# The down projection of a ViT tower layer in pairs of token blocks with seven block products, its fourth row sum on GpSimd

## The chip, the core and the metric

One core of one Trainium2 chip runs the whole program as one launch. The metric is the device time of one execution in microseconds (us), from its first to its last instruction and what lies around them. Three executions of the kernel before gave 1929.54, 1930.83 and 1933.36 us; their median, 1930.83 us, is the time before.

The engines are named as in the profile: PE (TensorE, matmuls) with PEld (its weight loads), DVE (VectorE), ACT (ScalarE), POOL (GpSimd), and SP (SyncE), whose queue issues the DMAs.

## What is computed

16 sequences of 128 tokens and 1024 features run through a state-space kernel, one attention block and one gated feed-forward block. The change is in the last step of the feed-forward block, the projection `down`:

```python
def _qlinear(x, q, scale, A, Bm):
    w = (q.astype(jnp.float32) - Q_ZERO) * (scale * Q_STEP)[:, None]
    y = jnp.einsum('bsh,oh->bso', x, w)
    return y + LR_SCALE * (x @ A @ Bm)
g = _qlinear(x, gate_q, gate_scale, gate_A, gate_B)
u = _qlinear(x, up_q, up_scale, up_A, up_B)
h = jax.nn.silu(g) * u
return _qlinear(h, down_q, down_scale, down_A, down_B)   # 2752 -> 1024, levels 0..15
```

The layer's output is that plus the residual `h1`.

## The kernel before

**Tiling.** `C` = 16 blocks of `P` = 128 tokens, n = 0 to 15. The 2752 hidden features are `IT` = 22 tiles of 128 rows, of which the first `FULL` = 21 come in two f16 parts (high and low, whose sum is the f32 value) and the last, half a tile with both parts stacked, in one. So a block is 43 weight tiles, and each is multiplied with the two halves of 512 output columns: 86 matmuls of 128x128 by 128x512 in f16. `levels[i]` is tile i of the quantised weights less 7.5, f16, held in SBUF in the rooms of `x_hi`, `x_lo` and `down_levels`. `parts[n % 3]` holds block n of the hidden values, 1376 KB, loaded from `hidden_parts` in DRAM.

**The stage.** Before it, the gate and up projections run as a loop over 42 jobs, each of which after the fourth is itself made of seven half products (`half_features`), with sums of tokens and of levels made by DVE, ACT and POOL beside the matmuls. The down stage then runs over n. PE does `down(n, ...)`: 86 matmuls into the two PSUM banks of `acc[n % 2]`, with `low_term(n)` (2 matmuls in f32, the low-rank term, to `ps_l`) in their midst, and raises `s_main`. ACT turns the low-rank term into `lrt[n % 2]` (`down_term`, line 1830). POOL adds the residual `h1d` to it (line 1162). DVE multiplies the sums by the column scales into `y[n % 2]` (line 2270) and adds `lrt` (line 2273), and SP stores `y`. In the last block the two halves of the columns come one after the other.

**Order.** Every engine's program is written out by hand; engines wait for one another by semaphores. PE starts block n when its parts have landed and DVE has read the bank (`s_y1`). SP loads parts n + 3 when block n's matmuls are done, then the residual n + 2, then stores y n. DVE reads operands either from PSUM (`acc`, `ps_l`) or from SBUF (all others); POOL works in SBUF alone. A helper `Chain` lets an instruction wait for the one before it on the same engine.

## Time and profile before

| | |
|---|---|
| median of 3 runs | 1930.83 us |
| the profiled execution's own time | 1929.66 us |
| its span, first to last instruction | 1927.9 us |
| PE busy | 1805.6 us, 94% of the span |
| DVE busy | 1197.5 us, 62% |
| POOL busy | 859.1 us, 45% |
| ACT busy | 712.6 us, 37% |
| down stage, first to last matmul | 1618.0 to 1923.9 us of the span |

Busy shares are means over stages that differ: in the down stage DVE, ACT and POOL have each less than an eighth of the time filled, in the gate and up stage POOL has more than half. In the rows below, a line such as `1667.27 18.58 PE acc L1514 x86` is a start time, a length, an engine, what it writes, the line of the kernel and the number of instructions taken together. "idle before" is the time for which the engine stood still ahead of an instruction, with what ended it.

### The profile page before, as it was taken

How to read it: one execution, taken by the hardware profiler on the slowest of the kernel's cores; microseconds unless marked ns; L12 is line 12 of the kernel's file. 1: busy time of each engine (PE TensorE's matmuls, PEld its weight loads, DVE VectorE, ACT ScalarE, POOL GpSimd, SP SyncE). 2: the span in 40 equal slices, each digit the busy share in tenths (PEclk: the TensorE clock that was granted, in tenths of full speed). 3: DMA queues.
4: the chain of work that ended last, by engine and by line, in shares of the span. 5: the costliest groups of instructions: out<-in, count | busy, mean ns of one | idle time of the engine just before them, and what ended most of it. 6: DMA issues, size and time to landing. Idle time of an engine off the chain costs nothing.

```text
span 1927.9 us, 31412 instructions
## 1 busy us (share of the span) xinstructions
PE 1805.6 (94%) x12892; PEld 984.2 (51%) x12892; DVE 1197.5 (62%) x1570; ACT 712.6 (37%) x1026; POOL 859.1 (45%) x593
## 2 busy tenths in 40 slices
PE   0586999999999999999999999999999999999999
PEld 0575665656666655545554344444444444444444
DVE  8996577787878888855656876675755554111111
ACT  4477243343433344432114645454544443000000
POOL 6973134343333434432361577664777774011111
PEclk9998999999999999999999999999999999999999
DMA  2122111111122221144532343434465454434341
GB/s 97 43 67 68 62 56 22 34 37 43 47 58 64 80 75 63 67 147 163 168 121 67 98 132 99 131 113 139 142 195 172 156 164 147 154 106 150 113 143 44
DMA packets 102704, 194.92 MB, mean 101 GB/s; under 512 B 14305, under 2 KB 75489, under 8 KB 92065
## 3 DMA queue, kind: packets, MB, share of 16 engines
q1 hardware_dynamic: 102560, 192.90, 31.2%
q8 instruction: 103, 1.69, 0.4%
q14 instruction: 41, 0.33, 0.1%
HBM read 135.72 MB, written 56.11 MB: 100 GB/s over the span
## 4 chain that ended last, share of the span: by engine, by line
PE 75%; DVE 9%; POOL 2%; issue 2%; ACT 2%; DMA 0%; DVEq 0%; ACTq 0%
PE acc L1514 15%; PE acc L1380 12%; PE acc L1382 12%; PE ps_p L1172 4%; PE ps_p L1174 4%; PE ps_p L1173 4%; PE acc L1286 3%; PE acc L1287 3%; PE ps_t L1199 3%; PE acc L1288 3%; PE ps_p L1188 2%; PE ps_p L1190 2%; PE ps_p L1189 2%; PE ps_l L1389 2%; POOL prob L1061 1%
## 5 line engine op out<-in xcount | busy, mean ns | idle before, releaser
L1061 POOL TENSOR_TENSOR prob<-prob,mx 128x1024 f32<-128x1024 f32 x64 | 121.4, 1897 | 371.5 <-DVE mx L1883 371.5
L1172 PE MATMUL ps_p<-x_hi,w_qk 128*128 128x512 f16 x512 | 194.7, 380 | 0.0
L1173 PE MATMUL ps_p<-x_lo,w_qk 128*128 128x512 f16 x512 | 194.0, 379 | 0.0
L1174 PE MATMUL ps_p<-x_hi,w_qk 128*128 128x512 f16 x512 | 194.0, 379 | 0.0
L2270 DVE TENSOR_TENSOR y<-acc,down_scale 128x1024 f32<-128x1024 f32 (+1 forms) x17 | 19.7, 1162 | 253.0 <-PE acc L1514 253.0
L1114 POOL TENSOR_TENSOR hidden<-up,hidden 128x512 f16<-128x512 f32 x80 | 91.1, 1160 | 144.8 <-ACT hidden L1740 144.6
L1162 POOL TENSOR_TENSOR lr_term<-lr_term,h_again 128x1024 f32<-128x1024 f32 x16 | 37.6, 2347 | 253.6 <-ACT lr_term L1830 253.6
L1188 PE MATMUL ps_p<-w_v,x_hi 128*128 128x256 f16 x512 | 140.5, 274 | 4.8 <-PEq L806 3.6
L1066 POOL TENSOR_TENSOR prob<-prob,sm 128x1024 f32<-128x1024 f32 x64 | 120.2, 1897 | 52.9 <-DVE sm L1890 52.9
L1189 PE MATMUL ps_p<-w_v,x_hi 128*128 128x256 f16 x512 | 140.4, 274 | 0.0
L1190 PE MATMUL ps_p<-w_v,x_lo 128*128 128x256 f16 x512 | 140.4, 274 | 0.0
L1574 ACT ACTIVATE pth<-ps_t 128x512 f16<-128x512 f32 x128 | 76.1, 595 | 163.8 <-PE ps_t L1199 163.7
L2135 DVE SCALAR_TENSOR_TENSOR up<-acc,gu_scale,up 128x512 f32<-128x512 f32 x120 | 90.0, 750 | 61.2 <-PE acc L1382 60.1
L258 PE MATMUL ssm_ps<-phase,magnitude 128*128 128x128 f32 x512 | 67.1, 288 | 65.0 <-DVE magnitude L469 61.9
L2135 DVE SCALAR_TENSOR_TENSOR gate<-acc,gu_scale,gate 128x512 f32<-128x512 f32 x120 | 89.6, 747 | 56.2 <-PE acc L1382 55.4
L1380 PE MATMUL acc<-x_hi,q_sums 128*128 128x512 f16 x320 | 121.7, 380 | 1.1 <-issue 0.8
L1380 PE MATMUL acc<-x_sum,q_sums 128*128 128x512 f16 x320 | 121.3, 379 | 0.0
L1382 PE MATMUL acc<-x_sum,q_sums 128*128 128x512 f16 x320 | 121.3, 379 | 0.0
L1380 PE MATMUL acc<-x_hi,q_f 128*128 128x512 f16 x320 | 121.3, 379 | 0.0
L1382 PE MATMUL acc<-x_lo,q_f 128*128 128x512 f16 x320 | 121.3, 379 | 0.0
L1382 PE MATMUL acc<-x_lo,q_sums 128*128 128x512 f16 x320 | 121.3, 379 | 0.0
L1894 DVE SCALAR_TENSOR_TENSOR ptl<-ps_t,pth 128x512 f16<-128x512 f32 x128 | 87.7, 685 | 47.4 <-ACT pth L1574 46.9
(343 smaller groups left out, 4367.7 us busy)
## 6 DMA issues: line engine op xcount, KB each, us to landing
q_raw<-in_gu_q SPq DMA_DIRECT2D x42, 1024.0 KB, 6.2
hid_parts<-hidden_parts SPq DMA_DIRECT2D x16, 1376.0 KB, 6.7
hidden_parts<-hidden SPq DMA_DIRECT2D x42, 512.0 KB, 3.5
down_raw<-in_down_q SPq DMA_DIRECT2D x22, 512.0 KB, 3.6
w_raw<-in_w_qk SPq DMA_DIRECT2D x8, 1024.0 KB, 5.0
h_tokens<-n_tok SPq DMA_DIRECT2D x16, 512.0 KB, 3.7
o_parts<-ot SPq DMA_DIRECT2D x32, 256.0 KB, 2.3
wv_raw<-in_w_o SPq DMA_DIRECT2D x8, 1024.0 KB, 4.8
```

The lines of the kernel that those rows point to most:

```text
L1061: nc.gpsimd.tensor_tensor(prob[s % 2][p][:], prob[s % 2][p][:], bc(mx[p][:], H, 2), ALU.subtract).then_inc(s_sub[p], 1)
L1066: nc.gpsimd.tensor_tensor(prob[s % 2][p][:], prob[s % 2][p][:], bc(sm[p][:], H, 2), ALU.mult).then_inc(s_prob[p], 1)
L1172: nc.tensor.matmul(out[:], w[:, j % 2, m, 0, at], xn_hi[:, k, tok], start=(k == 0), stop=False)
L1173: nc.tensor.matmul(out[:], w[:, j % 2, m, 0, at], xn_lo[:, k, tok], start=False, stop=False)
L1174: last = nc.tensor.matmul(out[:], w[:, j % 2, m, 1, at], xn_hi[:, k, tok], start=False, stop=(k == KT - 1))
L1188: nc.tensor.matmul(out, xn_hi[:, k, tok], wv[:, g % 2, 0, at], start=(k == 0), stop=False)
L1189: nc.tensor.matmul(out, xn_hi[:, k, tok], wv[:, g % 2, 1, at], start=False, stop=False)
L1190: last = nc.tensor.matmul(out, xn_lo[:, k, tok], wv[:, g % 2, 0, at], start=False, stop=(k == KT - 1))
L1380: nc.tensor.matmul(banks[bank], lev[:, k * P:(k + 1) * P], hi[:, k, :], start=(k == 0 and not adds), stop=False, skip_group_check=adds)
L1382: last = nc.tensor.matmul(banks[bank], lev[:, k * P:(k + 1) * P], lo[:, k, :], start=False, stop=(k == KH - 1), skip_group_check=adds)
L1514: last = nc.tensor.matmul(acc[n % 2][:, b, :], parts[n % 3][:, at], levels[i][:, b * CH:(b + 1) * CH], start=(i == 0 and part == 0), stop= ...
L2135: stt(to[:], banks[bank], scl[:, m, i:i + 1], to[:], ALU.mult, ALU.add).then_inc(s_read, 1)
```

## The change

Blocks 0 and 1 are done as before. Blocks 2 to 15 are done in seven pairs, q = 1 to 7, block n = 2q and block m = 2q + 1. Of the 22 tiles the first 20 are cut in two halves of `KD` = 10, the columns in two halves of 512, and the pair's 2 x 2 x 2 block products of these tiles are made from seven: p1, p2, p6, p5, p7, p3, p4, each 20 matmuls. The tiles 20 and 21 (3 matmuls for a block and half) are done plainly (`down_rest`): p22 is one of them, the others follow within p2, p3 and p4.

For that there are new sums. Of the levels, four per tile, made once (`level_sum`, in f16, 128x512): the first on DVE (ten), the third on POOL (ten), the second six on DVE and the last `BY_POOL` = 4 on POOL, the fourth on DVE (ten). Of the hidden values, four for each pair, in two pieces h of 128x640 in f32: the first and the third on POOL (`hid_one`, `hid_three`, three instructions a piece), the second on DVE (`sum_two_hid`, two a piece), the fourth on POOL (`hid_four`, two a piece, in place in the second's room). Each piece is then copied to a high f16 part by ACT (`high_hid_sum`) and its low part made by DVE (`low_hid_sum`). ACT also copies p1 to SBUF (`first_down`), so that p2 can be added to it in its bank. DVE reads the banks seven times a pair (c11, x22, v, x5, x7, c12, c21), and scaling is a step of its own for three of the four quarters.

There are four rooms for parts in place of three, one for the residual in place of two. In the last pair the columns' right half ends first. Two powers of two change in `hid_up` and `hid_down`; they move no instruction.

The diff, cut to its core:

```diff
...
+KD = 10
+DP = C // 2
...
+BY_POOL = 4
...
-            sp.dma_start(parts[n % 3][:], hid_dram[n, :, :]).then_inc(s_parts[n % 3], 16)
+            sp.dma_start(parts[n % 4][:], hid_dram[n, :, :]).then_inc(s_parts[n % 4], 16)
...
+        def next_residual(n):
+            sp.wait_ge(s_sum, n + 1)
+            sp.dma_start(h1d[:], h1_dram[n + 1, :, :]).then_inc(s_h1d, 16)
+        def store_rows(n):
             sp.wait_ge(s_y, n + 1)
             sp.dma_start(out[n, :, :], y[n % 2][:]).then_inc(s_yout[n % 2], 16)
...
+        for q in range(DP):
+            next_residual(2 * q)
+            if q + 2 < DP:
+                if q:
+                    sp.wait_ge(s_dprod, dprod(q, "p3"))
+                else:
+                    sp.wait_ge(s_main, 1)
+                load_parts(2 * q + 4)
+                if q:
+                    sp.wait_ge(s_dprod, dprod(q, "p4"))
+                else:
+                    sp.wait_ge(s_main, 2)
+                load_parts(2 * q + 5)
+            store_rows(2 * q)
+            if q + 1 < DP:
+                next_residual(2 * q + 1)
+                store_rows(2 * q + 1)
...
-        for n in range(C):
-            pool.wait_ge(s_h1d[n % 2], 16 * (n // 2 + 1))
+        def residual_and_term(n):
+            pool.wait_ge(s_h1d, 16 * (n + 1))
             pool.wait_ge(s_lrt, n + 1)
-            nc.gpsimd.tensor_tensor(lrt[n % 2][:], lrt[n % 2][:], h1d[n % 2][:], ALU.add).then_inc(s_sum, 1)
+            tt(lrt[n % 2][:], lrt[n % 2][:], h1d[:], ALU.add).then_inc(s_sum, 1)
+        def hid_one(q, h):
...
...
+            chain.after(tt(to[:], hid_piece(2 * q + 1, 0, h, 0), hid_piece(2 * q + 1, 1, h, 0), ALU.add))
+            chain.after(tt(to[:], to[:], hid_piece(2 * q + 1, 0, h, 1), ALU.add))
+            tt(to[:], to[:], hid_piece(2 * q + 1, 1, h, 1), ALU.add).then_inc(s_f1, 1)
+        def hid_three(q, h):
...
...
+            chain.after(tt(to[:], hid_piece(2 * q, 0, h, 0), hid_piece(2 * q + 1, 0, h, 0), ALU.subtract))
+            chain.after(tt(to[:], to[:], hid_piece(2 * q, 0, h, 1), ALU.add))
+            tt(to[:], to[:], hid_piece(2 * q + 1, 0, h, 1), ALU.subtract).then_inc(s_f3, 1)
+        def hid_four(q, h):
...
+            chain.after(tt(to[:], hid_piece(2 * q, 1, h, 0), to[:], ALU.subtract))
+            tt(to[:], to[:], hid_piece(2 * q, 1, h, 1), ALU.add).then_inc(s_f4, 1)
+        pool.wait_ge(s_prod, PROD.total)
+        for i in range(KD):
+            tt(level_sum(3, i), level_block(1, 1, i), level_block(0, 1, i), ALU.subtract).then_inc(s_l3, 1)
+        for q in range(DP):
+            if q:
+                hid_four(q, 0)
+                hid_four(q, 1)
+            if q + 1 < DP:
+                hid_one(q + 1, 0)
+                hid_one(q + 1, 1)
+                hid_three(q + 1, 0)
+            residual_and_term(2 * q)
+            if q == 0:
+                pool.wait_ge(s_half, 1)
+                for i in range(KD - BY_POOL, KD):
+                    pool.wait_ge(s_l1, i + 1)
+                    pool.wait_ge(s_l3, i + 1)
+                    tt(level_sum(2, i), level_sum(3, i), level_block(0, 0, i), ALU.add).then_inc(s_l2_pool, 1)
+            if q + 1 < DP:
+                hid_three(q + 1, 1)
+            residual_and_term(2 * q + 1)
...
+        down(1, 0, KD).then_inc(s_half, 1)
+        low_term(1)
+        down(1, KD, IT).then_inc(s_main, 1)
...
+        for q in range(1, DP):
+            n, m = 2 * q, 2 * q + 1
...
+            if q == 1:
+                pe.wait_ge(s_y1, 1)
+            else:
+                pe.wait_ge(s_dread, dread(q - 1, "c11"))
+            down_block(0, lambda i, part: hid_part(n, i, part), lambda i: level_block(0, 0, i), False, True).then_inc(s_dprod, 1)
             low_term(n)
...
-        low_term(C - 1)
...
+            if q == 1:
+                pe.wait_ge(s_y1, 2)
+            else:
+                pe.wait_ge(s_dread, dread(q - 1, "x22"))
+            down_rest(3, m, 1, False).then_inc(s_dprod, 1)
...
+            down_block(0, lambda i, part: hid_part(n, KD + i, part), lambda i: level_block(1, 0, i), True, False)
+            down_rest(0, n, 0, True).then_inc(s_dprod, 1)
+            pe.wait_ge(s_dl[1], 2 * q)
+            if q == 1:
+                pe.wait_ge(s_l2, KD - BY_POOL)
+                pe.wait_ge(s_l2_pool, BY_POOL)
+            else:
+                pe.wait_ge(s_dread, dread(q - 1, "c21"))
+            down_block(1, lambda i, part: dsum[1][part][:, i, :], lambda i: level_sum(2, i), False, True).then_inc(s_dprod, 1)
+            pe.wait_ge(s_dl[0], 2 * q)
+            if q == 1:
+                pe.wait_ge(s_l1, KD)
+            else:
+                pe.wait_ge(s_dread, dread(q - 1, "c12"))
+            down_block(2, lambda i, part: dsum[0][part][:, i, :], lambda i: level_sum(1, i), False, True).then_inc(s_dprod, 1)
+            pe.wait_ge(s_dl[2], 2 * q)
+            if q == 1:
+                pe.wait_ge(s_l3, KD)
+            pe.wait_ge(s_dread, dread(q, "v"))
+            down_block(1, lambda i, part: dsum[2][part][:, i, :], lambda i: level_sum(3, i), True, True).then_inc(s_dprod, 1)
+            pe.wait_ge(s_dl[3], 2 * q)
+            pe.wait_ge(s_dread, dread(q, "x5"))
+            down_block(2, lambda i, part: dsum[3][part][:, i, :], lambda i: level_block(1, 1, i), True, False)
+            down_rest(2, n, 1, True).then_inc(s_dprod, 1)
+            low_term(m)
+            if q == 1:
+                pe.wait_ge(s_l4, KD)
+            pe.wait_ge(s_dread, dread(q, "x7"))
+            down_block(1, lambda i, part: hid_part(m, KD + i, part), lambda i: level_sum(4, i), True, False)
+            down_rest(1, m, 0, True).then_inc(s_dprod, 1)
...
-        for n in range(C):
-            down_term(n)
+        def high_hid_sum(q, k, h, src, made):
+            act.wait_ge(made, 2 * (q - 1) + h + 1)
+            if q > 1:
+                act.wait_ge(s_dprod, dprod(q - 1, ("p5", "p6", "p7", "p3")[k]))
+            nc.scalar.activation(piece(dsum[k][0], h), src[:], ACT.Copy).then_inc(s_dh[k], 1)
+        def first_down(q):
+            act.wait_ge(s_dprod, dprod(q, "p1"))
+            if q > 1:
+                act.wait_ge(s_dread, dread(q - 1, "c21"))
+            nc.scalar.activation(first_d[:], acc[0][:, 0, :], ACT.Copy).then_inc(s_dfirst, 1)
+        act.wait_ge(s_prod, PROD.total)
+        for q in range(DP):
+            if q:
+                for h in two:
+                    high_hid_sum(q, 2, h, f3[h], s_f3)
+                first_down(q)
+            down_term(2 * q)
+            if q:
+                for h in two:
+                    high_hid_sum(q, 3, h, f2[h], s_f4)
+            if q + 1 < DP:
+                for h in two:
+                    high_hid_sum(q + 1, 1, h, f2[h], s_f2)
+                for h in two:
+                    high_hid_sum(q + 1, 0, h, f1[h], s_f1)
+            down_term(2 * q + 1)
...
+        def low_hid_sum(q, k, h, src):
+            dve.wait_ge(s_dh[k], 2 * (q - 1) + h + 1)
+            tt(piece(dsum[k][1], h), src[:], piece(dsum[k][0], h), ALU.subtract).then_inc(s_dl[k], 1)
+        def sum_two_hid(q, h):
...
+            dve.wait_ge(s_f1, 2 * (q - 1) + h + 1)
...
...
+            chain.after(tt(to[:], f1[h][:], hid_piece(2 * q, 0, h, 0), ALU.subtract))
+            tt(to[:], to[:], hid_piece(2 * q, 0, h, 1), ALU.subtract).then_inc(s_f2, 1)
+        def sum_down(q, name, product, bank, to, other, behind):
+            dve.wait_ge(s_dprod, dprod(q, product))
+            if behind:
+                dve.wait_ge(s_dread, dread(q, behind))
+            tt(to, banks[bank], other, ALU.add).then_inc(s_dread, 1)
...
+        def add_term(n, cols):
+            chain.wait()
             dve.wait_ge(s_sum, n + 1)
             tt(y[n % 2][:, cols], y[n % 2][:, cols], lrt[n % 2][:, cols], ALU.add).then_inc(s_y, 1)
+        def last_down(q):
+            sum_down(q, "c21", "p4", 1, y[1][:, left], first_d[:], None)
...
+            scaled(y[1], left)
...
+        dve.wait_ge(s_prod, PROD.total)
+        for i in range(KD):
+            tt(level_sum(1, i), level_block(0, 1, i), level_block(0, 0, i), ALU.subtract).then_inc(s_l1, 1)
         dve.wait_ge(s_dscl, 16)
         ts(scl_d[:], scl_d[:], down_scale[:], None, ALU.mult).then_inc(s_dscl2, 1)
+        dve.wait_ge(s_low, LOWS.total)
         dve.wait_ge(s_dscl2, 1)
-        for n in range(C - 1):
-            scale_sums(n, 0, False)
...
+        scale_sums(0)
+        for h in two:
+            sum_two_hid(1, h)
+        dve.wait_ge(s_half, 1)
+        for i in range(KD - BY_POOL):
+            dve.wait_ge(s_l3, i + 1)
+            tt(level_sum(2, i), level_sum(3, i), level_block(0, 0, i), ALU.add).then_inc(s_l2, 1)
+        scale_sums(1)
+        for k in (1, 0):
+            for h in two:
+                low_hid_sum(1, k, h, (f1, f2)[k][h])
+        add_first(0)
+        add_first(1)
+        for i in range(KD):
+            if i < KD - BY_POOL:
+                dve.wait_ge(s_l2, i + 1)
+            else:
+                dve.wait_ge(s_l2_pool, i + 1 - (KD - BY_POOL))
+            tt(level_sum(4, i), level_block(1, 0, i), level_sum(2, i), ALU.subtract).then_inc(s_l4, 1)
+        for q in range(1, DP):
+            if q > 1:
+                last_down(q - 1)
+                add_term(2 * q - 1, slice(0, D))
+            for h in two:
+                low_hid_sum(q, 2, h, f3[h])
+            for h in two:
+                low_hid_sum(q, 3, h, f2[h])
...
+            dve.wait_ge(s_dprod, dprod(q, "p2"))
+            tt(y[0][:, left], banks[0], scl_d[:, left], ALU.mult).then_inc(s_dread, 1)
...
+            sum_down(q, "x22", "p22", 3, y[1][:, right], first_d[:], None)
+            if q + 1 < DP:
+                sum_two_hid(q + 1, 0)
+            sum_down(q, "v", "p6", 1, y[0][:, right], first_d[:], None)
+            if q + 1 < DP:
+                sum_two_hid(q + 1, 1)
+                low_hid_sum(q + 1, 1, 0, f2[0])
+            sum_down(q, "x5", "p5", 2, y[1][:, right], y[1][:, right], "x22")
+            if q + 1 < DP:
+                for h in two:
+                    low_hid_sum(q + 1, 0, h, f1[h])
+                low_hid_sum(q + 1, 1, 1, f2[1])
+            sum_down(q, "x7", "p7", 1, y[1][:, right], y[1][:, right], "x5")
...
+            scaled(y[1], right)
+            sum_down(q, "c12", "p3", 2, y[0][:, right], y[0][:, right], "v")
...
+            scaled(y[0], right)
+            add_term(2 * q, slice(0, D))
+        add_term(C - 1, right)
+        last_down(DP - 1)
+        add_term(C - 1, left)
...
```

On DVE, in the first pair, this stands between the last hidden values of the gate and up stage and the first blocks' end before:

```order
L2193 TENSOR_TENSOR inner_stack1_2028<-ps_i1,inner_stack1_2028 32x512 [waits f_iact] x2
L2278 TENSOR_SCALAR down_scale_2038<-down_scale_2038,g_down_scale_1950 128x1024 [waits f_dscl]
L2270 TENSOR_TENSOR y0_2034<-acc0,down_scale_2038 128x1024 [waits f_main,f_dscl2]
L2273 TENSOR_TENSOR y0_2034<-y0_2034,lr_term0_2032 128x1024 [waits f_sum,f_y1]
L2270 TENSOR_TENSOR y1_2035<-acc1,down_scale_2038 128x1024 [waits f_main]
L2273 TENSOR_TENSOR y1_2035<-y1_2035,lr_term1_2033 128x1024 [waits f_sum,f_y1]
```

And now on DVE, from the second level sum (L2520) on; `hid_f20` and `hid_f21` are the two pieces of the second hidden sum, `hid_sum11` the low part of the second, `hid_sum21` of the third, L2532 the fourth level sum:

```order
L2520 TENSOR_TENSOR x_hi_64<-x_hi_64 128x512 [waits f_level_sum3] x5
L2462 TENSOR_TENSOR y1_2051<-acc1,down_scale_2053 128x1024 [waits f_main]
L2471 TENSOR_TENSOR hid_sum11_2036<-hid_f20_2043,hid_sum10_2035 128x640 [waits f_sum_hi2]
L2471 TENSOR_TENSOR hid_sum11_2036<-hid_f21_2044,hid_sum10_2035 128x640 [waits f_sum_hi2]
L2471 TENSOR_TENSOR hid_sum01_2034<-hid_f10_2041,hid_sum00_2033 128x640 [waits f_sum_hi1]
L2471 TENSOR_TENSOR hid_sum01_2034<-hid_f11_2042,hid_sum00_2033 128x640 [waits f_sum_hi1]
L2467 TENSOR_TENSOR y0_2050<-y0_2050,lr_term0_2048 128x1024 [waits f_sum,f_y1]
L2467 TENSOR_TENSOR y1_2051<-y1_2051,lr_term1_2049 128x1024 [waits f_sum,f_y1]
L2532 TENSOR_TENSOR x_lo_65<-x_lo_65,x_hi_64 128x512 [waits f_level_sum2] x6
L2532 TENSOR_TENSOR x_lo_65<-down_levels_2022,x_hi_64 128x512 [waits f_level_sum2_pool] x2
L2532 TENSOR_TENSOR x_lo_65<-down_levels_2022,x_lo_65 128x512 [waits f_level_sum2_pool] x2
L2471 TENSOR_TENSOR hid_sum21_2038<-hid_f30_2045,hid_sum20_2037 128x640 [waits f_sum_hi3]
```

The reading of block 1's bank (L2462) now stands behind the second level sums, and the low part for p7 (`hid_sum21`) behind all ten fourth level sums.

On POOL, at the end of the gate and up stage and the start of the down stage, before:

```order
L1118 TENSOR_SCALAR down_levels_2022<-down_raw_2023 128x1024 [waits g_lraw]
L1114 TENSOR_TENSOR hidden0_1975<-up01_1961,hidden0_1975 128x4x128 [waits g_hhi,d_xlo]
L1114 TENSOR_TENSOR hidden0_1975<-up00_1960,hidden0_1975 128x4x128 [waits g_hhi]
L1114 TENSOR_TENSOR hidden1_1976<-up11_1963,hidden1_1976 128x4x128 [waits g_hhi]
L1114 TENSOR_TENSOR hidden1_1976<-up10_1962,hidden1_1976 128x4x128 [waits g_hhi]
L1162 TENSOR_TENSOR lr_term0_2032<-lr_term0_2032,h1_again0_2036 128x1024 [waits f_lrt,f_h1d0]
L1162 TENSOR_TENSOR lr_term1_2033<-lr_term1_2033,h1_again1_2037 128x1024 [waits f_lrt,f_h1d1]
```

And now on POOL in an inner pair, from the end of the first hidden sum to the start of the next pair's fourth (`hid_f30` and `hid_f31` are the pieces of the third, `hid_f20` one of the fourth):

```order
L1234 TENSOR_TENSOR hid_f11_2042<-hid_f11_2042,hid_parts3_2032 128x640 [waits a_out0]
L1242 TENSOR_TENSOR hid_f30_2045<-hid_parts2_2031,hid_parts3_2032 128x640 [waits f_sum_lo3,f_parts2]
L1243 TENSOR_TENSOR hid_f30_2045<-hid_f30_2045,hid_parts2_2031 128x640 [waits a_out0]
L1244 TENSOR_TENSOR hid_f30_2045<-hid_f30_2045,hid_parts3_2032 128x640 [waits a_out0]
L1223 TENSOR_TENSOR lr_term0_2048<-lr_term0_2048,h1_again_2052 128x1024 [waits f_lrt,f_h1d]
L1242 TENSOR_TENSOR hid_f31_2046<-hid_parts2_2031,hid_parts3_2032 128x640 [waits f_sum_lo3,f_parts2]
L1243 TENSOR_TENSOR hid_f31_2046<-hid_f31_2046,hid_parts2_2031 128x640 [waits a_out0]
L1244 TENSOR_TENSOR hid_f31_2046<-hid_f31_2046,hid_parts3_2032 128x640 [waits a_out0]
L1223 TENSOR_TENSOR lr_term1_2049<-lr_term1_2049,h1_again_2052 128x1024 [waits f_lrt,f_h1d]
L1251 TENSOR_TENSOR hid_f20_2043<-hid_parts2_2031,hid_f20_2043 128x640 [waits f_parts2,f_sum_lo2]
```

A queue that held one instruction a block now holds nine a block; the residual's addition stands between the two pieces of the third sum.

## Rows read from the trace of the kernel before

**Rows 1.** The page: engine, busy us (share) xinstructions; then busy tenths in 40 slices.
```profile
PE 1805.6 (94%) x12892; PEld 984.2 (51%) x12892; DVE 1197.5 (62%) x1570; ACT 712.6 (37%) x1026; POOL 859.1 (45%) x593
...
PE   0586999999999999999999999999999999999999
```

**Rows 2.** Chain that ended last, in order of time, down stage: start, us, what.
```profile
1633.05 0.45 PE ps_l L1526 x2
...
1648.22 18.58 PE acc L1514 x86
1666.80 0.47 PE ps_l L1526 x2
```

**Rows 3.** The same chain's end.
```profile
1910.08 13.85 PE acc L1514 x64
1923.92 0.02 issue
1923.95 0.70 DVE y L2270
```

**Rows 4.** Busy time by stretch; a busy time (xcount) for each engine, clock, DMA.
```profile
core 0: us, PE busy (x) PEld busy (x) DVE busy (x) ACT busy (x) POOL busy (x), PEclk, DMA share, GB/s
182.00:191.00 9.00, 3.57 (x16) 2.77 (x14) 2.61 (x3) 4.63 (x7) 0.00 (x0) 0.50 0.06 25
191.00:195.00 4.00, 3.24 (x16) 2.35 (x17) 2.56 (x5) 0.00 (x0) 0.00 (x0) 0.50 0.55 180
196.00:200.00 4.00, 4.00 (x39) 3.59 (x38) 2.50 (x2) 0.60 (x1) 0.00 (x0) 1.00 0.05 4
1648.00:1905.00 257.00, 257.00 (x1189) 117.61 (x1189) 31.93 (x27) 15.60 (x14) 32.87 (x14) 1.00 0.36 119
```

**Rows 5.** Groups by line and shape: count | busy, mean ns | idle before.
```profile
L1162 POOL TENSOR_TENSOR lr_term<-lr_term,h_again 128x1024 f32<-128x1024 f32 x16 | 37.6, 2347 | 253.6 <-ACT lr_term L1830 253.6
L2273 DVE TENSOR_TENSOR y<-y,lr_term 128x1024 f32<-128x1024 f32 x15 | 18.4, 1225 | 0.5
L2273 DVE TENSOR_TENSOR y<-y,lr_term 128x512 f32<-128x512 f32 x2 | 1.4, 692 | 0.1
L2278 DVE TENSOR_SCALAR down_scale<-down_scale,g_down_scale 128x1024 f32<-128x1024 f32 x1 | 0.8, 753 | 1.1 <-DMA down_scale<-in_down_scale 1.1
L1830 ACT ACTIVATE lr_term<-ps_l,g_down_back 128x1024 f32<-128x1024 f32 x16 | 17.8, 1114 | 263.6 <-PE ps_l L1526 263.6
```

**Rows 6.** Lines of the gate and up stage: min/median/max ns.
```profile
L1106 POOL TENSOR_TENSOR q_sums<-q_f x40: 1145/1154/1163, 1064.4 to 1600.2; 128x512 f16<-128x512 f16 x40
L1747 ACT ACTIVATE x_sum<-sum x24: 612/619/631, 1030.1 to 1284.2; 128x512 f16<-128x512 f32 x24
L2175 DVE TENSOR_TENSOR sum<-sum,x_hi x8: 681/1159/1639, 1038.2 to 1262.4; 128x512 f32<-128x512 f32 x8
```

**Rows 7.** Timeline, POOL, gate and up stage: start, us, instruction.
```profile
1151.94 1.16 POOL L1108 TENSOR_TENSOR q_sums<-q_f 128x512 f16<-128x512 f16 x1
1153.05 1.60 POOL L1109 TENSOR_TENSOR q_sums<-q_f,q_sums 128x512 f16<-128x512 f16 x1
```

**Rows 8.** The same stretch on DVE.
```profile
1152.03 0.75 DVE L2135 SCALAR_TENSOR_TENSOR up<-acc,gu_scale,up 128x512 f32<-128x512 f32 x1 [0.32 <-PE acc L1382]
1152.70 0.94 DVE L2154 TENSOR_TENSOR x_sum<-sum,x_sum 128x512 f16<-128x512 f32 x1
1153.56 1.64 DVE L2175 TENSOR_TENSOR sum<-sum,x_hi 128x512 f32<-128x512 f32 x1
1155.23 0.69 DVE L2176 TENSOR_TENSOR sum<-sum,x_lo 128x512 f32<-128x512 f32 x1
```

**Rows 9.** Timeline, DVE, first stage: a 640-element instruction, and one beside POOL.
```profile
67.65 0.82 DVE L459 TENSOR_TENSOR phase<-a,c_im 128x640 f32<-128x640 f32 x1
68.39 2.95 DVE L465 TENSOR_TENSOR v_second<-w_v 128x1024 f32<-128x1024 f32 x1
```

**Rows 10.** DMA issues of the down stage: xcount, KB each, median us to landing.
```profile
hid_parts<-hidden_parts SPq DMA_DIRECT2D x15, 1376.0 KB, 6.6
```

**Rows 11.** Timeline, PE, 181 to 192: matmuls after an idle time.
```profile
186.17 1.97 PE L275 MATMUL n_pn<-ident,magnitude 128*128 128x128 f32 x8 [2.57 <-ACT magnitude L342]
191.76 0.37 PE L1188 MATMUL ps_p<-w_v,x_hi 128*128 128x256 f16 x1 [3.62 <-PEq L806]
```

131 lines of the change are left out of this document (92 added, 39 removed).

## The prediction, as it stood before the run

> **What bounds the kernel now.** Read the page first: PE is busy for 94% of the span and for nine tenths or more of every slice after the fourth [rows 1]. Then the chain of waits in order of time: through the down stage it is PE alone, 86 matmuls in 18.58 us and two f32 ones of the low-rank term in 0.47 us, block after block [rows 2], so 0.216 us a matmul and 38.10 us for two blocks. The busy times by stretch say the same: 257 us of 257 for PE at the full clock, and 31.9 us for DVE, 15.6 for ACT, 32.9 for POOL [rows 4]. Only the number of matmuls can shorten this stage, as long as the other three keep up. The last matmul starts 0.38 us before 1923.92; behind it lie DVE's two instructions of 0.7 us and a store [rows 3].
>
> **What is removed.** A pair takes 7 x 20 + 3 + 3 x 3 = 152 matmuls where two blocks took 172, and the same 4 f32 ones: 152 x 0.216 + 2 x 0.47 = 33.8 us for 38.1. Seven pairs: 140 x 0.216 = **30.2 us less**. That part is certain.
>
> **What is added, per inner pair.** POOL: 16 instructions of 640 elements and the two additions of 1024. One of 512 takes 1.154 us [rows 6], one of 1024 2.347 [rows 5], so one of 640 1.45, and 16 x 1.45 + 2 x 2.35 = 27.9 us, with some 0.8 us between chained ones. DVE: 12 of 640 from SBUF at 0.82 [rows 9], three scalings of 512 at 0.69 and two additions of 1024 at 1.23 [rows 5], seven readings of a bank at about 0.69: 9.8 + 2.1 + 2.5 + 4.8 = 19.2 us. ACT: 8 copies of 640 at about 0.72 (0.62 for 512 [rows 6]), one of 512 and two of 1024 at 1.11 [rows 5]: 8.6 us. Each alone fits into 33.8 us. If that were all, the work would hide behind PE.
>
> **What speaks against it: DVE and POOL stop one another.** In the gate and up stage POOL's L1108 ends at 1153.10 [rows 7]. DVE's L2154, begun at 1152.70, has two SBUF operands and takes 0.94 in place of 0.68 us [rows 8]. POOL's next takes 1.60 in place of 1.16 [rows 7], and DVE's next, L2175, 1.64 [rows 8] where its shortest is 0.681 [rows 6]. They take turns: from POOL's end at 1153.10 to its next at 1154.65 are 1.55 us, of which POOL works some 1.02 and DVE 0.53. L2135, one of whose operands is in PSUM, is not held up beside the same POOL instructions: 0.75 [rows 8]. The first stage shows it again, 2.95 us for an instruction of 1024 elements [rows 9]. In the down stage it is not seen, because POOL and DVE have one short instruction each a block, at different times. The change puts 17 DVE instructions with two SBUF operands into each pair beside 18 of POOL.
>
> The Trainium skill has this as a rule (SBUF — State Buffer, section SBUF: two separate sides): the port pair that the two share is taken for a whole instruction, and the loser fully blocks. By the rule's letter a turn of two 512s would be 1.16 + 0.69 = 1.85 us, where the trace shows 1.55; the measurement decides, and with 1.85 the sum below would be some 30 us higher.
>
> Scaled to 640 elements a turn is 1.31 + 0.68 = **1.99 us**, the price of each of the 12 while POOL is kept busy. An addition of 1024 costs 1.08 + 1.31 = 2.4 us, a scaling between 0.69 and 1.9, say 1.2. DVE's inner pair is then 12 x 1.99 + 2 x 2.4 + 3 x 1.2 + 7 x 0.61 (readings back to back) = 36.6 us, and 0.8 us of waits for POOL that find no filler: **37.4 us**. POOL's is about the same, 16 turns of 1.99 and the additions. So neither hides behind 33.8 us; PE waits ahead of p3 and p4, whose banks DVE has to read first. Five inner pairs (q = 2 to 6): **17.9 us more**. The last pair has no next one to prepare, and runs at PE's pace. The bounds: with 1.40 and 0.78 us for the 640s a pair is 36.2, with 1.50 and 0.82 it is 38.2, so 12 to 22 us.
>
> **The first pair.** Zero is the first down matmul, 1618.0. I lay DVE's queue out from there. POOL makes the ten third level sums until 16, waits for parts 3, which SP issues at 8 behind other loads (6.6 us and more to landing [rows 10]), until about 20, and has the first piece at 24.6. DVE then does four instructions of the second hidden sum, with a wait of 1.4 for the second piece (to 34.0), six level sums f16 from f16 in turns with POOL (9.9), block 1's bank (1.2), four low parts (7.8, one behind an addition of POOL's), the additions of blocks 0 and 1 (4.8), ten fourth level sums (14.5, eight in turns), four low parts (5.4), two bank readings (1.2), two sums for pair 2 (3.7) and v (0.6): it ends at **83.0**. p7 waits for v. At PE's pace p7 would start at 39.05 + 4.3 + 0.5 + 0.6 + 5.0 + 4.3 + 4.3 = 58.1. Of the 25.0 us between, 1.3 are lost ahead of p22 (block 1's bank), 4.9 ahead of p2 (ACT's copy of p1 stands behind the high part of the third sum's second piece, which POOL finishes at 48.6) and 18.8 ahead of p7. With 1.6 us ahead of p3: **26.6 us more**.
>
> An f16 level sum alone is not in the trace. Between 0.38 (half of DVE's 1024 elements of one operand in 0.753 [rows 5]) and 0.69 for two [rows 5] I take the middle, 0.53, as no row is nearer; the ends are 2.4 us less and 3.0 more. The Trainium skill (VectorE: DVE Perf Modes, section The perf-mode tier table) gives two-operand 16-bit instructions in SBUF twice the rate; an estimate from its formula is 0.42 us, and the sum would be 1.8 us lower. No run here shows it yet. Landings 1 us a load sooner or later move this pair by 2 us down or 4 up.
>
> **The clock.** After 9 us in which PE was busy for 3.57, and a wait of 3.62 us [rows 4, 11], the granted clock stood at 0.50 from 191 to 195 and at 1.00 from 196 [rows 4]. A wait of 18.8 us should do that at least once: about 4 us at half pace, **2 us**, between 0 and 4.
>
> **The tail.** p4 is followed by three DVE instructions where two stood, 0.7 us, and its bank is the last: with the hand-overs **1.0 us**.
>
> **The sum.** -30.2 + 17.9 + 26.6 + 2.0 + 1.0 = **+17.3 us**. The profiled execution took 1929.66 us, 1.2 under the median; 1947.0 on that, **1948** on the median of 1930.83. The loss is made in the first pair, and the inner pairs gain only 0.7 us each on what stood before (37.4 for 38.1).
>
> **Rivals.**
> *The engines don't stop one another here.* Faster. If turns cost nothing, DVE's 19 and POOL's 28 us hide, and the first pair has only 3 us of waits, for parts 3 and POOL's sums: -30.2 + 3 + 1 = -26, 1905 us. For it: each engine's own sum is under 33.8. Against it: rows 7 to 9, in two stages. Its point of decision is the low parts' duration, 0.82 or about 2 us. 7%.
> *The turns are real, but half hidden.* If POOL's waits for landings and for the low-rank term leave DVE free, an inner pair is 35 and the first one 52: -30.2 + 6 + 18 + 2 = -4, 1927. For it: POOL has 8 to 9 us of waits in the first pair. Against: they fall at its end, behind the queue. 11%, half of it faster by over 0.2%, half the same.
> *POOL is the bound.* If its instructions on strided f16 pieces take 1.6 us, or three and more turns fall into one addition, an inner pair is 40 and the first 66: -30.2 + 31 + 32 + 4 + 1 = +38, 1969. For it: nothing in [rows 6], where a strided form is absent. 9%.
> *It doesn't do what it says.* The two new powers of two and the rooms move no instruction, and the order of the instructions shows the seven products; under 1%, in the others.
>
> **How the numbers follow.** My forecast has 73% and on its own reaches from 1936 (lower ends of the turns and of the f16 sums, no clock loss) to 1961 (upper ends of all). The range 1932 to 1961 leaves out the fast rival, most of the second and the third. Within 0.2%, 3.9 us, a measurement of this kernel can't tell a change. Faster 0.13, same 0.07, slower 0.80: the forecast, the POOL rival, and below 1935 a little of the forecast's own tail.
>
> **What would show it.** In the profile after: low parts (L2471) at a mean of 1.6 us or more with a least of about 0.82, and POOL's 640s at 1.8 to 1.9 with a least of 1.45; p1 to p1 (from one wait to the next on L1652) 37 us in the inner pairs and 34 in the last; PE idle for 15 us or more once, about 64 us after the first down matmul, ended by DVE; DVE filled nearly without gaps there. Low parts near 0.82 throughout would say that the first rival is right; inner pairs at 33.8 with a slow first pair, that the second is; an idle time of PE ended by POOL or a DMA, that I have the wrong queue.

## The result, and the profile after

The changed kernel takes **1941.66 us** (median of 6 runs, 1938.19 to 1944.73) where the kernel before takes 1930.52 beside it (6 runs, 1929.54 to 1933.36): ratio 1.0054, 95% interval 1.0042 to 1.0065. It is slower by 11 us. The forecast was 1948, between 1932 and 1961. The profiled execution took 1941.62 us, its span is 1939.7.

The page of the changed kernel: engine, busy us (share) xinstructions, then busy tenths in 40 slices of 48.5 us; against [rows 1].

```profile
PE 1786.0 (92%) x12752; PEld 973.8 (50%) x12752; DVE 1430.6 (74%) x1735; ACT 753.7 (39%) x1089; POOL 1088.6 (56%) x719
...
PE   0586999999999999999999999999999999699998
...
DVE  8996477787878888855657876765755555989996
...
POOL 6973134333333334432361667655776867979994
PEclk9998999999999999999999999999999999899999
```

140 matmuls are gone. From the 35th slice on DVE is at 8 or 9 of ten and POOL at 7 or 9, until the last pair, where in the down stage of before each had about an eighth of the time filled [rows 4]; PE's 35th slice, at 6, is the first pair. Busy times by stretch (columns as in [rows 4]): the first pair, an inner pair, the last pair.

```profile
1660.15:1717.35 57.20, 39.70 (x157) 16.71 (x156) 51.40 (x40) 8.90 (x12) 44.83 (x25) 0.79 0.28 107
1717.35:1753.90 36.55, 34.08 (x157) 15.42 (x156) 35.32 (x24) 8.12 (x11) 35.77 (x19) 1.00 0.40 136
1900.90:1934.80 33.90, 33.90 (x157) 15.37 (x155) 18.64 (x18) 4.06 (x5) 12.62 (x6) 1.00 0.21 78
```

The first pair takes 57.2 us at a mean clock of 0.79; from its end at 1717.35 to the last pair's start at 1900.92 are 183.6 us, 36.7 for each of the five inner pairs, with DVE busy for 35.3 and POOL for 35.8 of the 36.55 us shown; the last pair has PE's own pace. PE's timeline in the first pair (start, us, instruction, idle before it):

```profile
1664.93 0.82 PE L1661 MATMUL acc<-down_levels,hid_parts 128*128 128x512 f16 x3
1669.05 5.30 PE L1652 MATMUL acc<-x_lo,hid_parts 128*128 128x512 f16 x12 [3.29 <-ACT first_down L2014]
...
1681.16 4.48 PE L1652 MATMUL acc<-x_hi,hid_sum 128*128 128x512 f16 x20
1699.85 5.28 PE L1652 MATMUL acc<-x_hi,hid_sum 128*128 128x512 f16 x12 [14.21 <-DVE y L2488]
1704.92 4.78 PE L1652 MATMUL acc<-x_lo,hid_sum 128*128 128x512 f16 x20
```

The granted clock behind the two waits (busy times by stretch; it is the third figure from the end):

```profile
1669.00:1672.00 3.00, 2.95 (x7) 1.04 (x8) 3.00 (x2) 0.00 (x0) 3.00 (x2) 0.50 0.00 0
...
1699.00:1703.00 4.00, 3.15 (x8) 1.17 (x9) 3.97 (x5) 0.74 (x1) 3.84 (x3) 0.50 0.42 135
```

From p22's end (1664.93 + 3 x 0.216) to p2 are 3.47 us, from p5's end (1681.16 + 20 x 0.216) to p7 14.37. Behind each wait twelve matmuls take 5.3 us, 0.43 each, at a granted clock of 0.50, the lower of its two levels (1.2 GHz), where twenty take 4.48 at the higher one. The 23 matmuls of p2 take 7.79 us in place of 4.97, those from p7 to the pair's end 17.50 in place of 14.73: 5.6 us. Together 23.4 us, the whole of 57.2 - 33.8. What DVE does before p7 (its timeline):

```profile
1663.66 7.64 DVE L2471 TENSOR_TENSOR hid_sum<-hid_f,hid_sum 128x640 f16<-128x640 f32 x4
...
1675.91 9.31 DVE L2532 TENSOR_TENSOR x_lo<-x_lo,x_hi 128x512 f16<-128x512 f16 x6
1685.13 3.14 DVE L2532 TENSOR_TENSOR x_lo<-down_levels,x_hi 128x512 f16<-128x512 f16 x2
1688.20 0.74 DVE L2532 TENSOR_TENSOR x_lo<-down_levels,x_lo 128x512 f16<-128x512 f16 x2
...
1699.03 0.68 DVE L2488 TENSOR_TENSOR y<-acc,first_down 128x512 f32<-128x512 f32 x1
```

Four low parts take 7.64 us, 1.9 from one start to the next. Eight fourth level sums (L2532) follow at 1.54 from start to start, and the last two, when POOL waits, at 0.33, each 0.41 long. The reading v ends at 1699.7, and PE starts p7 behind it. In the inner pairs, groups by line (xcount | busy, mean ns | idle before). L2471 makes a low part, L2498 adds the residual and the low-rank term, L2493 scales, L1233 is a step of a hidden sum on POOL and L2488 reads a bank:

```profile
L2471 DVE TENSOR_TENSOR hid_sum<-hid_f,hid_sum 128x640 f16<-128x640 f32 x40 | 78.1, 2000 | 0.0
L2498 DVE TENSOR_TENSOR y<-y,lr_term 128x1024 f32<-128x1024 f32 x10 | 23.1, 2311 | 0.3
L2493 DVE TENSOR_TENSOR y<-y,down_scale 128x512 f32<-128x512 f32 x15 | 21.9, 1459 | 0.5
L1233 POOL TENSOR_TENSOR hid_f<-hid_f,hid_parts 128x640 f32<-128x640 f32 x10 | 18.6, 1861 | 0.8
L2488 DVE TENSOR_TENSOR y<-acc,y 128x512 f32<-128x512 f32 x15 | 10.2, 678 | 0.0
```

DVE's instructions with two SBUF operands are stretched: a low part takes 2.00 us for 0.82 [rows 9], an addition 2.31 for 1.23 and a scaling 1.46 for 0.69 [rows 5]. Those that read a bank (L2488) are not, 0.678. The chain of waits of an inner pair (start, us, what) runs through a load:

```profile
1827.13 0.66 PE acc L1661 x3
...
1827.81 6.72 DMA hid_parts<-hidden_parts
...
1834.60 1.65 POOL hid_f L1232
...
1844.08 1.88 POOL hid_f L1234
...
1845.98 2.02 DVE hid_f L2480
...
1859.29 4.49 PE acc L1652 x20
1863.78 0.66 PE acc L1661 x3
```

p4 ends. A block's parts are loaded (6.8 us), POOL makes the first sum's six instructions (11.4), DVE the second sum and the low parts up to the reading x7 (13.3), and then comes p4 of that pair (5.2). Whether this loop or the time that the two engines share sets the 36.7 is asked of the last two experiments.

### The profile page after: what moved, and what is told of

It is laid out like the page before. It is cut to its first block, busy times and chain, and to the rows that moved or that the text cites. A ratio compares the mean times of both kernels' runs of the same rounds, so it can differ in the third digit from the quotient of the medians.

```text
span 1939.7 us, 31648 instructions
## 1 busy us (share of the span) xinstructions
PE 1786.0 (92%) x12752; PEld 973.8 (50%) x12752; DVE 1430.6 (74%) x1735; ACT 753.7 (39%) x1089; POOL 1088.6 (56%) x719
## 4 chain that ended last, share of the span: by engine, by line
PE 62%; DVE 13%; POOL 6%; issue 3%; DMA 3%; ACT 2%; POOLq 0%; DVEq 0%; ACTq 0%; SPq 0%
PE acc L1492 12%; PE acc L1494 12%; PE ps_p L1284 4%; PE ps_p L1286 4%; PE ps_p L1285 4%; PE acc L1652 3%; PE acc L1398 3%; PE acc L1400 3%; PE acc L1399 3%; PE ps_t L1311 3%; PE ps_p L1300 2%; PE ps_p L1301 2%; PE ps_p L1302 2%; DVE hid_sum L2471 2%; DMA hid_parts<-hidden_parts 2%
## 5 line engine op out<-in xcount | busy, mean ns | idle before, releaser
L1900 ACT ACTIVATE gate<-gate 128x512 f32<-128x512 f32 (+1 forms) x88 | 55.1, 626 | 135.9 <-DVE gate L2331 133.3
L2471 DVE TENSOR_TENSOR hid_sum<-hid_f,hid_sum 128x640 f16<-128x640 f32 x56 | 101.8, 1867 | 0.0
```

The source lines that it names most:

```text
L2471: tt(piece(dsum[k][1], h), src[:], piece(dsum[k][0], h), ALU.subtract).then_inc(s_dl[k], 1)
```

## Experiments

Times are medians beside the kernel before on the same chip, whose own median was 1931.0 to 1932.5 us. "First pair" and "inner pairs" are read from the starts of p1 on PE's timeline.

**1. GpSimd's work without its length.** The kernel leaves out most of each hidden sum from pair 2 on.

```diff
+NARROW = 16
...
+        def cut(q, tile):
+            return tile[:, :, 0:NARROW] if q > 1 else tile[:, :, :]
...
-            to = f1[h]
...
+            to = cut(q, f1[h])
...
```

> From pair 2 on, every GpSimd instruction of a hidden sum works on 16 of the 128 tokens of each tile (80 elements a partition in place of 640); their number, their waits and everything else stay. Most of each sum is thus left out, and the output is not the layer's. DVE's instructions are unchanged. If the two engines take turns (my theory), DVE's 640s of pairs 3 to 7 fall from 1.87 to near 0.82 us, DVE's busy time in an inner pair from 35 to about 22 us, and the inner pairs from 36.7 to PE's 33.8 us: 14.5 us less. Pair 1's second half loses its turns too (its fourth level sums go to 0.37-0.4 us each as the two shortest of after did), 8 to 11 us less. In all 1915 to 1920 us. If DVE's instructions are long by themselves (operand forms, f16 output) and POOL has nothing to do with it, they stay at 1.87 and the pairs at 36.7: 1941. If the load of the parts and the chain of hand-overs set the pair, it falls by less than 1 us a pair.

It takes 1918.21 us (one run; the kernel before takes 1932.47). The first pair is 47.2 us, the inner pairs are 33.77. Groups by line on DVE from 1680 to 1880:

```profile
L2475 DVE TENSOR_TENSOR hid_sum<-hid_f,hid_sum 128x640 f16<-128x640 f32 x48 | 38.1, 836 | 12.9 <-ACT hid_sum L2012 12.2
L2492 DVE TENSOR_TENSOR y<-acc,y 128x512 f32<-128x512 f32 x18 | 12.4, 691 | 34.0 <-PE acc L1665 21.3 <-PE acc L1656 12.7
```

The low parts fall from 2.00 to 0.84 us with DVE's program and every hand-over unchanged, and DVE now waits for ACT and PE. That GpSimd's instructions stretch VectorE's is shown. The inner pairs' whole loss goes, and 10 us of the first one's. GpSimd's own sums are shorter too, so how the loss divides between the two engines this run alone doesn't tell.

**2. The fourth sum back on VectorE** (the part that the title names, undone alone).

```diff
-            if q:
-                hid_four(q, 0)
-                hid_four(q, 1)
...
+            for h in two:
+                hid_four(q, h)
```

> The fourth sum's four instructions a pair are made by VectorE, at the start of the pair ahead of the low parts, in place of GpSimd: that part of the change alone is undone. In turns, a 640 costs 1.31 us of the shared time on POOL and 0.68 on DVE, so moving four saves 2.5 us a pair of it, while DVE gets 4 x 0.82 = 3.3 us of its own work more. Theory (the shared time is the bound, both engines being busy for 35 of 36.7 us): an inner pair gets shorter by 0.5 to 2.5 us, say 36.0, and the first by 1 to 3: 1936 us (1929 to 1939). Rival (VectorE's own queue is the bound, as its 35 busy us suggest, and GpSimd only stretches it here and there): 3.3 us a pair more, 1955 to 1960.

It takes 1937.66 us, ratio 1.0027 (1.0014 to 1.0039), 4 us less than the changed kernel and inside the expectation. The first pair is 54.3, the inner pairs 36.4. VectorE got 3.3 us of work a pair more and the pair got shorter, so the rival, 1955 or more, is out. But of 2.5 us of shared time saved only 0.3 arrive. POOL now waits for the load in every inner pair, 7.4 to 10.4 us (its timeline):

```profile
1830.40 1.81 POOL L1232 TENSOR_TENSOR hid_f<-hid_parts 128x640 f32<-128x640 f16 x1 [8.58 <-DMA hid_parts<-hidden_parts]
```

**3. The fourth level sums behind x5 of pair 1.**

```diff
-        for i in range(KD):
...
-            tt(level_sum(4, i), level_block(1, 0, i), level_sum(2, i), ALU.subtract).then_inc(s_l4, 1)
...
             sum_down(q, "x5", "p5", 2, y[1][:, right], y[1][:, right], "x22")
+            if q == 1:
+                for i in range(KD):
...
```

> The ten fourth level sums of VectorE stand behind the reading x5 of pair 1 in place of ahead of pair 1's low parts; nothing is added or left out. PE's wait ahead of p7 (14.2 us) was for v behind them. Theory (the whole queue of VectorE sets the first pair, since it is filled without gaps from the second sum to x7): p7 starts some 13 us sooner, and PE waits ahead of p3 or p4 in its place, for x7 or the fourth level sums; the pair gets 1 to 3 us shorter, pair 2 begins with its sums late; 1939 us (1936 to 1942). Rival (the place of the sums is the loss, and p7's wait with its slow clock simply goes): 14.2 + 2.8 us less, 1925.

It takes 1943.46 us, ratio 1.0052 (1.0033 to 1.0072): no gain. PE's timeline:

```profile
1690.22 4.24 PE L1652 MATMUL acc<-x_hi,hid_sum 128*128 128x512 f16 x12 [5.32 <-DVE y L2488]
1697.39 2.75 PE L1652 MATMUL acc<-x_lo,hid_sum 128*128 128x512 f16 x12 [1.21 <-DVE y L2488]
1713.26 6.38 PE L1652 MATMUL acc<-x_lo,hid_parts 128*128 128x512 f16 x20 [10.29 <-DVE y L2488]
```

One wait of 14.2 has become 5.3, 1.2 and 10.3, with slow matmuls behind two of them. The rival falls: the place of the ten sums is not the loss. My own expectation missed too. The first pair got 2.0 us longer (59.2), not 1 to 3 shorter. PE stands still in it for 20.6 us in place of 17.8; the slow matmuls behind three waits cost 5.0 us, no more than the 5.6 behind two. Where the 2.8 us come from was not asked. The second pair got 0.9 shorter.

**4. p1's copy ahead of the second high part.**

```diff
-                for h in two:
-                    high_hid_sum(q, 2, h, f3[h], s_f3)
-                first_down(q)
+                high_hid_sum(q, 2, 0, f3[0], s_f3)
+                if q == 1:
+                    first_down(q)
+                high_hid_sum(q, 2, 1, f3[1], s_f3)
...
```

> In pair 1 ScalarE copies p1 between the two high pieces of the third sum, not behind them; nothing else. The wait ahead of p2 (3.3 us, and 2.8 us lost at half clock behind it) goes. Theory (p7's start is set by VectorE's queue, so waits ahead of it are not added up): p7 begins when it did, its wait grows from 14.2 to about 20 us, and the time is the same, 1941 us within 2. Rival (as my prediction's sum had it, each wait a term of its own): 6 us less, 1935.5.

It takes 1941.08 us, ratio 1.0045 (1.0027 to 1.0062). The wait ahead of p2 is gone and that ahead of p7 has grown by as much (PE's timeline):

```profile
1697.23 5.28 PE L1652 MATMUL acc<-x_hi,hid_sum 128*128 128x512 f16 x12 [20.50 <-DVE y L2491]
```

The first pair is 57.10 us for 57.20. So only the time at which VectorE's queue reaches v counts, and the rival, 6 us less, is out.

**5. All hidden sums and second level sums on VectorE, in a new order.** A table of steps takes the place of the written order. `one0` is the first sum's piece 0 and so on, `low3x` and `low4x` are this pair's low parts, `low1x` and `low2x` the next one's; Y is c11 with x22, V v, X x5, S x7 and T c12 with their scalings; L2, LA and LB are level sums, B block 1's bank, A the two additions.

```diff
-BY_POOL = 4
+BY_POOL = 0
+START = """one0 three0 one1 two0 L2 two1 three1 low10 low20 B A low11 low21"""
+PAIR_ONE = """four0 one0 Y four1 low30 low40 low31 V two0 low41 one1 two1 LA low20 low10 X S LB low11 three0 T three1 low21"""
+PAIR = """four0 four1 low30 Y low31 one0 V low40 one1 low41 three0 X two0 S two1 three1 low10 T low20 low11 low21"""
```

> All hidden sums (16 instructions of 640 a pair) and all second level sums on VectorE; GpSimd keeps the ten third level sums and the two additions of the residual a pair. VectorE's steps of a pair stand in a new order: four steps of the fourth sum, the high-priority readings c11, x22, v, x5, x7, c12 as soon as their products can be there, low parts and the next pair's sums between them, and the fourth level sums behind v of pair 1. VectorE's own work in an inner pair: 28 x 0.836 (as in the kernel with narrow GpSimd sums) + 7 x 0.68 + 3 x 0.69 + 2 x 1.22 = 32.7 us, with at most 2 x 2.1 us of GpSimd's two additions between. Theory (the shared time is what counts: 28 x 0.68 + 2 x 2.1 + 3.8 = 27 us in place of 37, and VectorE is not stopped outside the two additions): inner pairs 33.8 to 35.5, first pair 38 to 43, 1904 to 1917 us, faster than both kernels. Rival (VectorE alone is too full, 32.7 of 33.8 with every hand-over on it): inner pairs 36.5 to 38 and the first 45, 1925 to 1935.

It takes **1911.86 us**, ratio 0.9896 (0.9881 to 0.991): less than both kernels. Busy times of the second pair:

```profile
1699.70:1733.50 33.80, 33.80 (x158) 15.44 (x156) 31.76 (x41) 8.79 (x12) 4.71 (x2) 1.00 0.43 147
```

DVE's low parts (group by line, 1700 to 1880), and PE's only wait, on its timeline:

```profile
L2429 DVE TENSOR_TENSOR hid_sum<-hid_f,hid_sum 128x640 f16<-128x640 f32 x42 | 34.1, 833 | 0.0
```

```profile
1686.53 5.28 PE L1611 MATMUL acc<-x_lo,hid_sum 128*128 128x512 f16 x12 [5.77 <-DVE y L2475]
```

VectorE does 16 instructions a pair more than in the changed kernel and is busy for less: 31.8 us in place of 35.3. The first pair is 42.6 us, the inner ones 33.8.

**6. The same work in the old order.**

```diff
+PAIR = """four0 four1 low30 low31 low40 low41 Y three0 three1 one0 two0 V one1 two1 low20 X low10 low11 low21 S T"""
```

`PAIR_ONE` is the same, and the fourth level sums stand at the end of `START`.

> The same distribution of work (all hidden sums and second level sums on VectorE), with VectorE's steps in the order of the changed kernel: the fourth sum at a pair's start, the third of the next pair behind x22, the first ahead of the second, the fourth level sums ahead of pair 1. It tells the engine from the order. Theory (order matters when VectorE is within 2 us of full, because v, x5 and x7 stand behind six to twelve instructions that don't concern them): inner pairs 36 to 37.5, first pair 45 to 48, 1925 to 1932 us. Rival (only the amount of shared time counts): as the kernel in the new order, 1904 to 1917.

It takes 1940.83 us, ratio 1.0047 (1.0032 to 1.0062). The order is worth 29 us. That is more than expected: the time was to be 1925 to 1932, and the inner pairs are 38.4, not 36 to 37.5. One of them, on PE's timeline:

```profile
1809.00 4.44 PE L1611 MATMUL acc<-x_hi,hid_sum 128*128 128x512 f16 x12 [2.59 <-DVE y L2475]
```

The stretch behind that wait, with the granted clock at 0.50:

```profile
1811.00:1813.00 2.00, 2.00 (x6) 0.67 (x5) 1.93 (x4) 0.00 (x0) 0.00 (x0) 0.50 0.00 0
```

Between c11 with x22 and v stand 11 instructions of 0.82 us. PE loses 2.8 us to it, and 1.7 more at half clock. In an inner pair of the changed kernel no wait is longer than 1.9 us and no matmul is slow. So what the cheaper work gained was given back by order and clock.

**7. Only pair 1's sums on VectorE.**

```diff
...
-            if q + 1 < DP:
+            if 0 < q < DP - 1:
                 hid_one(q + 1, 0)
...
```

> Only pair 1's hidden sums (16 instructions) and the second level sums are VectorE's; from pair 2 on everything is as in the changed kernel. Theory (in the first pair VectorE's queue sets the end, and every instruction of GpSimd beside it costs its queue more than doing the work itself: 1.31 us of turn against 0.83): the first pair falls from 57.2 to 46 to 51 us, the inner ones stay at 36.7; 1931 to 1936 us. Rival (VectorE's queue gets 16 x 0.83 = 13 us longer and GpSimd's idle time brings nothing back): 1950 or more.

It takes 1932.52 us, ratio 1.0004 (0.9994 to 1.0013), as long as the kernel before. The first pair is 48.1, the inner pairs 36.7. VectorE's queue got 20 instructions longer, four of them level sums, and yet p7 began 31.0 us after p1 in place of 39.7.

**8. The old order with its readings moved forward.**

```diff
-... three0 three1 one0 two0 V one1 two1 low20 X low10 low11 low21 S T"""
+... three0 three1 V one0 two0 X one1 two1 S low20 low10 low11 low21 T"""
```

> The kernel with all sums on VectorE in the old order, and one thing moved in every pair: v, x5 and x7 stand 5, 6 and 4 instructions of 0.82 us earlier on VectorE (v right behind the third sum, x5 behind the second's first piece, x7 ahead of the low parts). No instruction is added or left out. In the old order PE waits 2.6 us ahead of p7 for v in each inner pair, and its next twelve matmuls then take 4.4 us in place of 2.75. Theory (order, and the half clock that a wait of that length brings): without that wait no slow matmuls either; inner pairs 34.5 to 36 us in place of 38.2, first pair 42 to 45; 1916 to 1926 us. Rival (VectorE is simply full in these pairs and what is moved ahead of one wait comes back at the next): inner pairs 37.5 or more, 1936 to 1941.

It takes 1920.06 us, ratio 0.9934 (0.9912 to 0.9957), 21 us less than experiment 6 for three moved readings. The first pair is 43.9, the inner pairs are 33.8, 33.8, 34.6, 35.5 and 35.5. PE's longest wait in the inner pairs is 1.14 us, and the twelve matmuls behind it take 2.75. The rival, that VectorE is simply full and the pairs stay at 37.5 or more, is out; in the last two, though, VectorE is busy for 34.9 of the 35.5 us.

**9. The new order, refined.**

```diff
-PAIR_ONE = """four0 one0 Y four1 low30 low40 low31 V two0 low41 one1 two1 LA low20 low10 X S LB low11 three0 T three1 low21"""
+PAIR_ONE = """one0 low30 Y four0 one1 low31 four1 low40 V low41 two0 two1 LA X three0 low10 LB low11 S T low20 low21 three1"""
```

> The fastest kernel so far with another order of VectorE's steps, chiefly in pair 1: x5 stands right behind the first five fourth level sums and ahead of the next pair's first low parts, and the third sum's low part is made ahead of the fourth sum. There PE waited 5.8 us ahead of p3 for x5, and lost 2.6 us more at half clock. Theory: the wait shrinks to 2 us or less and the slow matmuls go with it; the first pair 36 to 39 us in place of 42.6, inner pairs 33.8 as before; 1904 to 1909 us. Rival (the first pair is bound by the sum of VectorE's work since the second sum, which is unchanged): 1911 to 1912.

It takes **1909.03 us**, ratio 0.9876 (0.9856 to 0.9895), the least of all, though its interval and that of experiment 5 overlap. PE's timeline in the first pair, which is 37.9 us where it was 42.6:

```profile
1678.45 2.75 PE L1611 MATMUL acc<-x_hi,hid_sum 128*128 128x512 f16 x12 [1.34 <-DVE y L2475]
1684.64 2.75 PE L1611 MATMUL acc<-x_lo,hid_sum 128*128 128x512 f16 x12 [1.72 <-DVE y L2475]
```

These are the two longest waits, 3.1 us together, with no slow matmul behind either. `START` and `PAIR` were changed slightly as well; the inner pairs are 34.1, so those changes did not help.

**10 and 11. Loop or shared time?** x7 and its scaling ahead of the three low parts, in the changed kernel and in that of experiment 2.

```diff
+            sum_down(q, "x7", "p7", 1, y[1][:, right], y[1][:, right], "x5")
...
             if q + 1 < DP:
                 for h in two:
                     low_hid_sum(q + 1, 0, h, f1[h])
                 low_hid_sum(q + 1, 1, 1, f2[1])
-            sum_down(q, "x7", "p7", 1, y[1][:, right], y[1][:, right], "x5")
```

> The changed kernel with one move: the reading x7 (and its scaling) stands ahead of the three low parts of the next pair that were ahead of it, in every pair. In the chain of waits of an inner pair, these low parts stand between the load of a block's parts (issued when p4 is done), GpSimd's first sum, VectorE's second sum and the next p4: a loop of 6.7 + 11.4 + 13.3 + 5.2 = 36.6 us. Theory A (this loop through the load sets the inner pair): without 5.9 us of low parts in it the pairs get shorter, down to 34 to 35.5 us, and the time falls by 6 to 13 us, to 1929 to 1936. Theory B (VectorE's and GpSimd's shared time sets it, and the loop only fits itself to that, for both are busy for 35.7 of 36.6 us): PE's wait moves to another product, the inner pairs stay at 36 to 37 us on average, 1938 to 1942.

> The same move of x7 in the kernel that makes the fourth sum on VectorE, where GpSimd waits 8.6 us in each inner pair for the load. Theory A (there the loop through the load is the bound; that kernel's pairs are 36.2 us though its shared time is 2.5 us a pair less): the inner pairs fall to about 34 to 35 us, 1926 to 1932 us. Theory B (no gain, shared time or VectorE's own work is the bound there too): 36.2 and 1937 us as before.

With the move the changed kernel takes 1939.22 us, ratio 1.0045 (1.003 to 1.006), and its inner pairs 36.5 on average, as theory B (the shared time) had it. One of them, of 38.2, has 1.6 us of slow matmuls in it. The kernel of experiment 2 takes 1933.91, ratio 1.0015 (1.0006 to 1.0025), and its inner pairs 35.7 for 36.4. That lies between its two theories: A (the loop) had 34 to 35, B no gain. Busy times of the five inner pairs of experiment 10:

```profile
1714.00:1897.00 183.00, 171.56 (x783) 77.33 (x782) 176.24 (x119) 40.27 (x55) 177.74 (x91) 0.99 0.37 129
```

And of experiment 11:

```profile
1714.60:1893.00 178.40, 169.79 (x781) 76.76 (x780) 174.17 (x140) 40.15 (x55) 138.12 (x70) 1.00 0.38 131
```

In experiment 10 POOL never waits for the load in an inner pair, so the loop is open. POOL is at 97%, DVE at 96%, and the pair is all but as long. So the loop in the chain of waits merely fitted the pair; what is left as the bound of the changed kernel is the shared time, which experiments 1 and 5 speak for. With the fourth sum on VectorE the move saves 0.7 us a pair, and then DVE is full, at 98%.

## Why the prediction was right, and where its sizes were off

| term, us | forecast | measured | from |
|---|---|---|---|
| 140 matmuls | -30.2 | -30.2 | 12892 - 12752 |
| inner pairs | +17.9 | +14.6 | 5 x (36.71 - 33.8) |
| waits in the first pair | +26.6 | +17.8 | 3.47 + 14.37 |
| clock | +2.0 | +5.6 | 2.82 + 2.77 |
| tail | +1.0 | +0.9 | 4.86 behind the last matmul for 3.98 |
| ahead of pair 1 | 0 | +3.1 | first down matmul at 1620.97 for 1617.99, and 0.1 that the other rows leave |
| sum | +17.3 | +11.8 | spans 1939.7 and 1927.9 |

The sum came out nearer than its terms did, and that is in part luck: the two large terms were too high by 3.3 and 8.8 us, and the clock and the row ahead of pair 1 too low by 3.6 and 3.1.

**Bound, and what is removed:** as forecast. **The turns:** right, shown by experiment 1. The low parts have a mean of 2.00 us in the inner pairs and a least of 0.81; POOL's 640s mostly take 1.86, with a least of 1.39. A turn is 1.95 us from one POOL start to the next (1842.13 to 1844.08) where I took 1.99, an addition of 1024 takes 2.31 for 2.4. A scaling takes 1.46, more than my 1.2. DVE is busy for 35.4 us of an inner pair where I summed 36.6, above all because the first step of the second sum (L2480) takes 1.65 in the mean, once in a pair 0.82; it is idle for 1.3, of which 0.9 are waits for POOL, where I had 0.8. So **the inner term was 0.7 us a pair too high**. By the rule that I had cited, of the Trainium skill (SBUF — State Buffer, section SBUF: two separate sides), a turn would be the two whole instructions, 1.46 + 0.82 = 2.28 us. The trace shows less, 1.95, as it did before the change (1.55 for 1.85), and 12 turns at 2.28 would, by estimate, make the pair 4 us longer than it is.

**The first pair:** the right queue and the right reading. v was to end 83.0 us after the first down matmul and ended at 78.7. What was off is the sizes on that queue: POOL's first two pieces came 1.4 and 1.5 us sooner, the fourth level sums took 13.0 us for 14.5, the second ones 9.2 for 9.9, and the rest is tenths. A 16-bit level sum alone takes 0.41 us, near my range's lower end of 0.38 and not 0.53; the 0.42 that I had named beside it fits. The waits of 1.3 ahead of p22 and 1.6 ahead of p3 did not come. That the waits may be read as one sum up to v, and not one by one, is what experiments 3 and 4 show.

**The clock:** the term that I made too small. I priced one slow stretch, behind p7's wait. There was one behind p2's 3.3 us as well, and each cost 2.8, not 2.

**Ahead of the stage:** the start of the stage moves by itself. With the same code ahead of it, it is at 1618.36 in experiment 4 and at 1621.75 in experiment 3, and over all experiments between 1617.96 and 1622.44. The kernel before has one trace, with 1617.99. So the 3 us may be chance, but that is not shown: without this row the others give +8.7, where the medians differ by 11.1 (the profiled executions by 12.0). What makes the other 2.4 is open.

**The rivals.** No mutual stopping: it is out, the low parts are at 2.00. Half hidden: it is out by the inner pairs, 36.7 and not 35; the first pair, 57.2, lies between its 52 and my 62.4. POOL as the bound: POOL is filled to 94 to 98% in the inner pairs, but a 640 takes it 1.40 us when DVE leaves it alone, not 1.6, and the pairs are 36.7 us, not 40.
